# A graph-attention layer and a mixture-of-experts FFN in one kernel: bias and carry matmuls over 128 rows, both square roots behind a relu, two buffers of high halves, two one-hot buffers

## The reference, cut to what matters

```python
x = x + gnn(layernorm(x), edge_attr, W, att_src, att_dst, src, dst)
x = x + ffn(layernorm(x), Wr, br, W1, ..., Wo, bo)

def gnn(feat, dist, ...):                      # 4 heads of 64
    ft = (feat @ W).reshape(n, 4, 64)
    e  = leaky_relu(sum(ft * att_src)[src] + sum(ft * att_dst)[dst], 0.2)
    ex = exp(e - segment_max(e, dst)[dst])
    a  = ex / segment_sum(ex, dst)[dst] * dist
    return segment_sum(ft[src] * a, dst)

def ffn(x, ...):                               # 8 experts, every node goes through all
    w = softmax(x @ Wr + br)
    h = relu(bn(x @ W1[e] + b1[e])); h = relu(bn(h @ W2[e] + b2[e]))
    return sum over e of (h @ Wo[e] + bo[e]) * w[:, e]
```

## Time and profile before

| what | value |
|---|---|
| time, median of 3 runs | 1561.23 us (1560.53 to 1564.69) |
| profiled execution: first to last instruction | 1556.4 us |
| TensorE matmuls busy | 1485.0 us, 95% of the span |
| VectorE busy | 1231.7 us, 79% |
| GpSimd busy | 1063.0 us, 68% |
| ScalarE busy | 742.2 us, 48% |
| mean granted TensorE clock | 0.985 |

### The profile page before, as it was taken

How to read it: one execution, slowest core, us unless ns; L and a number is a source line. 1 busy time by engine, 2 the same in 40 slices (tenths; PEclk the granted TensorE clock), 3 DMA queues, 4 the chain that set the end, 5 groups by cost and what they waited for, 6 DMA issues and landing times.

```text
span 1556.4 us, 24165 instructions
## 1 busy us (share of the span) xinstructions
PE 1485.0 (95%) x8478; PEld 1298.3 (83%) x8478; DVE 1231.7 (79%) x2302; ACT 742.2 (48%) x1293; POOL 1063.0 (68%) x951
## 2 busy tenths in 40 slices
PE   6928999999999999999999999999999999999998
PEld 4727888878888888888888888888888888888887
DVE  7746787887788888878888888888888888888751
ACT  3500444444455555545555555554555555555543
POOL 4176767777778777777777877777777787787000
PEclk9959999999999999999999999999999999999999
DMA  8776344353543444353344444434334444443000
GB/s 239 203 233 192 110 137 124 106 141 94 144 121 111 122 126 127 103 142 108 103 135 118 112 119 118 128 106 137 108 107 134 119 111 119 129 111 91 18 7 8
DMA packets 106070, 187.50 MB, mean 120 GB/s; under 512 B 38357, under 2 KB 70490, under 8 KB 105919
## 3 DMA queue, kind: packets, MB, share of 16 engines
q0 software_dynamic: 44688, 123.13, 28.5%
q1 hardware_dynamic: 60701, 62.29, 13.9%
q10 hardware_dynamic: 560, 0.52, 0.1%
HBM read 172.72 MB, written 14.42 MB: 120 GB/s over the span
## 4 chain that ended last, share of the span: by engine, by line
PE 82%; DVE 9%; DMA 3%; issue 2%; ACT 2%; POOL 1%; SPq 0%; DVEq 0%; ACTq 0%
PE bankH L831 39%; PE bankY L860 21%; PE bankE L783 5%; PE bankE L784 5%; PE bankB L761 3%; PE bankE L776 2%; DVE gath L1431 1%; POOL gath L675 1%; DVE msg_lo L1437 1%; ACT h L1030 1%; DMA table<-gath 1%; PE bankA L808 1%; DVE x L1506 1%; DMA gath<-table,src_win 1%; PE bankA L799 1%
## 5 line engine op out<-in xcount | busy, mean ns | idle before, releaser
L675 POOL DMA_INDIRECT gath<-table,src_win x900 | 1042.5, 1158 | 336.0 <-issue 245.2
L1030 ACT ACTIVATE h<-bankH,bn_shift,bn_scale 128x250 f32<-128x250 f32 x800 | 400.9, 552 | 314.9 <-PE bankH L831 314.7
L831 PE MATMUL bankH<-h,w 128*128 128x250 f32 x1600 | 380.5, 380 | 2.8 <-ACT h L1030 2.1
L860 PE MATMUL bankY<-wo,h 128*125 128x256 f32 x1600 | 378.4, 379 | 1.1 <-DVE x L1506 1.1
L831 PE MATMUL bankH<-xT,w 128*128 128x250 f32 x1600 | 370.9, 374 | 0.3 <-ACT h L1030 0.3
L860 PEld LDWEIGHTS bankY<-wo,h 128*125 128x125 f32 x1600 | 296.1, 187 | 43.2 <-issue 1.4
L831 PEld LDWEIGHTS bankH<-h,w 128*128 128x128 f32 x1600 | 295.6, 191 | 43.4 <-issue 9.6
L831 PEld LDWEIGHTS bankH<-xT,w 128*128 128x128 f32 x1600 | 296.7, 190 | 32.2 <-ACT h L1030 0.4
L1437 DVE TENSOR_TENSOR msg_lo<-gath,msg_hi 128x2340 fp32r<-128x2340 f32 x90 | 234.3, 2603 | 88.0 <-ACT msg_hi L1002 88.0
L1002 ACT ACTIVATE msg_hi<-gath 128x2340 fp32r<-128x2340 f32 x90 | 193.8, 2154 | 217.0 <-PE bankE L784 192.0
L1506 DVE SCALAR_TENSOR_TENSOR x<-bankY,gate,x 125x256 f32<-125x256 f32 x400 | 173.9, 476 | 116.7 <-PE bankY L860 116.1
(11 more groups left out here) (190 smaller groups left out, 1027.6 us busy)
## 6 DMA issues: line engine op xcount, KB each, us to landing
onehot_t<-dst_low SPq DMA_DIRECT2D x48, 576.0 KB, 5.9
gath<-table,src_win POOLq DMA_INDIRECT x900, 2.9
x_res<-in_x SPq DMA_DIRECT2D x25, 250.0 KB
out<-x SPq DMA_DIRECT2D x25, 250.0 KB
table<-gath SPq DMA_DIRECT2D x25, 227.5 KB
w<-in_L_ffn_W SPq DMA_DIRECT2D x8, 512.0 KB
gath<-in_x SPq DMA_DIRECT2D x5, 672.0 KB
wo<-in_L_ffn_Wo SPq DMA_DIRECT2D x4, 512.0 KB
```

The costliest lines, as they stand in the source:

```text
L675: pool.indirect_dma_start(gath[:, g.slot(u), t, :], None, table, bass.IndirectOffsetOnAxis(src_win[:, g.win, u, t:t + 1], 0)).then_inc(row ...
L831: mm = pe.matmul(target[:, hc * 2 * NT:(hc + 1) * 2 * NT], weights[:, e * KC + c, hc * P:(hc + 1) * P], operand(c), start=(c == 0), stop=( ...
L860: mm = pe.matmul(bankY[0:NT, u * D:(u + 1) * D], h2[:, e % 2, c, u, :], wo[:, e * KC + c, :], start=(c == 0), stop=(c == KC - 1))
L1030: ins = act.activation(target[:, e % 2, hc, :, :].rearrange("p u n -> p (u n)"), source[:, hc * 2 * NT:(hc + 1) * 2 * NT], ACT.Relu, bias= ...
```

## The change

- `out_bias` and `turn_carry` work over 128 partitions. `gate_t`, `bo_rows` and `row_max` get 128 rows; the rows that hold nothing are filled once at the start. The carry's transposes now have 128 moving columns instead of 8.
- In the last residual's stage, ScalarE runs relu of layer 2 first and then both `root1`.
- `msg_hi` has two buffers. `keep_high` waits for the chunk before the last one that was split, and `low_part`, whose `msg_lo` still has one buffer, waits for the last one.
- The one-hots have two buffers. Chunks 0 and 1 of pair a are built in stage 7, chunks 2 and 3 of pair g itself in the stages 4 and 5 (3 and 4 in pair 0), each when the chunk two before it has been summed. The code calls these `late`.

```diff
+HOTS = 2
+HIGHS = 2
-NEXT = {4: (0,), 5: (1,), 6: (2,), 7: (3,)}
+NEXT = {7: (0, 1)}
+LATE = {4: (2,), 5: (3,)}
-STEADY = Plan(FOUR, new=2, onehots={4: (0,), 5: (1,), 7: (2, 3)}, residuals={6: (0, 1)}, passes=((0, (0, 1)),), low=ALL)
-PLANS = {0: Plan({2: (0,), 3: (1,), 5: (2,), 6: (3,)}, place=2, new=5, rows=5, onehots={3: (0, 1), 7: (2, 3)},
+STEADY = Plan(FOUR, new=2, onehots=NEXT, late=LATE, residuals={6: (0, 1)}, passes=((0, (0, 1)),), low=ALL)
+PLANS = {0: Plan({2: (0,), 3: (1,), 5: (2,), 6: (3,)}, place=2, new=5, rows=5, onehots={7: (0, 1)}, late={3: (2,), 4: (3,)},
...
-         1: Plan({3: (0,), 4: (1,), 6: (2, 3)}, new=6, rows=6, onehots={4: (0,), 6: (1,), 7: (2, 3)},
+         1: Plan({3: (0,), 4: (1,), 6: (2, 3)}, new=6, rows=6, onehots={7: (0, 1)}, late={4: (2,), 5: (3,)},
...
-def last_low(g, c):
+def low_before(g, c, back):
     for order in reversed(range(g.n * CHUNKS + c)):
         if order % CHUNKS in plan_of(Pair(order // CHUNKS)).low:
-            return order + 1
+            back -= 1
+            if back == 0:
+                return order + 1
     return None
...
-        bo_rows = sb("bo_rows", [4 * EX, D], F32R)
+        bo_rows = sb("bo_rows", [P, D], F32R)
-        onehot = sb("onehot", [P, CHUNKS, TC, NT], F32R)
-        msg_hi = sb("msg_hi", [P, TC, ROW], F32R)
+        onehot = sb("onehot", [P, HOTS, TC, NT], F32R)
+        msg_hi = sb("msg_hi", [P, HIGHS, TC, ROW], F32R)
-        row_max = sb("row_max", [SEG, 2 * P])
+        row_max = sb("row_max", [P, 2 * P])
-        gate_t = sb("gate_t", [4 * EX, 2, NT], F32R)
+        gate_t = sb("gate_t", [P, 2, NT], F32R)
...
-                    mm = pe.transpose(bankC[:, way * SEG:(way + 1) * SEG], row_max[:, way * P:(way + 1) * P], ident[0:SEG, 0:SEG])
+                    mm = pe.transpose(bankC[:, way * P:(way + 1) * P], row_max[:, way * P:(way + 1) * P], ident[:, :])
...
-                if last_low(g, c) is not None:
-                    act.wait_ge(agg_done, last_low(g, c))
+                if low_before(g, c, HIGHS) is not None:
+                    act.wait_ge(agg_done, low_before(g, c, HIGHS))
...
-                    if g is not None and s == max(plan.residuals):
-                        root1(g, 0)
-                        if f is None:
-                            root1(g, 1)
                     if g is not None and s == plan.turn:
                         keep_x1T(g)
                     if run and (s >= 1 or not f.begins(1)):
                         relu2(*before(f, s, 1))
-                    if f is not None and g is not None and s == max(plan.residuals):
+                    if g is not None and s == max(plan.residuals):
+                        root1(g, 0)
                         root1(g, 1)
...
+            own.did(dve.memset(gate_t[:].bitcast(F32), 0.0))
+            own.did(dve.memset(bo_rows[:].bitcast(F32), 0.0))
...
-                if order >= CHUNKS:
-                    dve.wait_ge(agg_done, order + 1 - CHUNKS)
+                if order >= HOTS:
+                    dve.wait_ge(agg_done, order + 1 - HOTS)
...
                 dve.wait_ge(hi_ready, lows(g, c) + 1)
+                if low_before(g, c, 1) is not None:
+                    dve.wait_ge(agg_done, low_before(g, c, 1))
...
-                for c in range(CHUNKS):
+                for c in range(HOTS):
                     make_onehot(a, c)
...
+                    if g is not None:
+                        for c in plan.late.get(s, ()):
+                            make_onehot(g, c)
```

More of the change, by code:

```diff
@@ L87, with __init__ @@
 class Plan:
-    def __init__(self, sums, place=1, bounds=3, new=1, rows=3, onehots=None, residuals=None, products=None, passes=(), low=()):
+    def __init__(self, sums, place=1, bounds=3, new=1, rows=3, onehots=None, late=None, residuals=None, products=None, passes=(), low=()):
         self.sums, self.place, self.bounds, self.new, self.rows, self.onehots = sums, place, bounds, new, rows, onehots
         self.residuals, self.passes, self.low, self.turn = residuals, passes, low, 7
+        self.late = late
         self.products = products or {s - 1: chunks for s, chunks in sums.items()}
@@ L775, in aggregate @@
                     for t in range(TC):
-                        mm = pe.matmul(bankE[u][0:NT, 0:ROW], onehot[:, c, t, :].bitcast(F32), gath[:, g.slot(u), cols + t, :],
+                        mm = pe.matmul(bankE[u][0:NT, 0:ROW], onehot[:, c % HOTS, t, :].bitcast(F32), gath[:, g.slot(u), cols + t, :],
                                        start=(cols + t == 0), stop=(cols + t == TE - 1))
@@ L781, in aggregate @@
                 u, cols = c // 2, (c % 2) * TC
+                high = msg_hi[:, lows(g, c) % HIGHS, :, :]
                 for t in range(TC):
-                    pe.matmul(bankE[u][0:NT, 0:ROW], onehot[:, c, t, :], msg_hi[:, t, :], start=(cols + t == 0), stop=False)
-                    mm = pe.matmul(bankE[u][0:NT, 0:ROW], onehot[:, c, t, :], msg_lo[:, t, :], start=False, stop=(cols + t == TE - 1))
+                    pe.matmul(bankE[u][0:NT, 0:ROW], onehot[:, c % HOTS, t, :], high[:, t, :], start=(cols + t == 0), stop=False)
+                    mm = pe.matmul(bankE[u][0:NT, 0:ROW], onehot[:, c % HOTS, t, :], msg_lo[:, t, :], start=False, stop=(cols + t == TE - 1))
                 mm.then_inc(agg_done, 1)
@@ L998, in keep_high @@
                 act.wait_ge(msg_ready, g.n * CHUNKS + c + 1)
-                if last_low(g, c) is not None:
-                    act.wait_ge(agg_done, last_low(g, c))
+                if low_before(g, c, HIGHS) is not None:
+                    act.wait_ge(agg_done, low_before(g, c, HIGHS))
                 cols = (c % 2) * TC
-                act.activation(msg_hi[:], gath[:, g.slot(c // 2), cols:cols + TC, :], ACT.Copy).then_inc(hi_ready, 1)
+                act.activation(msg_hi[:, lows(g, c) % HIGHS, :, :], gath[:, g.slot(c // 2), cols:cols + TC, :], ACT.Copy).then_inc(hi_ready, 1)
             def exp_logits(g, k, tiles):
@@ L1023, in keep_gate @@
                 act.wait_ge(gateT_done, f.n + 1)
[L1024 removed]
+                act.activation(gate_t[0:4 * EX].rearrange("e u n -> e (u n)"), bankA[0:4 * EX, 256:256 + 2 * NT], ACT.Copy).then_inc(gateT_kept, 1)
             def relu(f, e, l, done, target, source):
@@ L1213, in aside @@
                     own.settle()
-                    dve.scalar_tensor_tensor(bo_rows[:], bo_high.bitcast(F32), bo_pick[:, 1:2], bo_low, ALU.mult, ALU.add).then_inc(bo_ready, 1)
+                    dve.scalar_tensor_tensor(bo_rows[0:4 * EX], bo_high.bitcast(F32), bo_pick[:, 1:2], bo_low, ALU.mult, ALU.add).then_inc(bo_ready, 1)
                 if n == 19:
@@ L1406, in logits @@
                 ends = prefix[:, :, 0:TE:TE - 1]
-                own.did(dve.tensor_tensor(ends, ends, bankC[:, 0:2 * SEG].rearrange("p (k s) -> p s k", k=2), ALU.max))
+                own.did(dve.tensor_tensor(ends, ends, bankC[:, 0:2 * P].rearrange("p (k s) -> p s k", k=2)[:, 0:SEG, :], ALU.max))
                 own.settle()
@@ L1435, in low_part @@
                 dve.wait_ge(hi_ready, lows(g, c) + 1)
+                if low_before(g, c, 1) is not None:
+                    dve.wait_ge(agg_done, low_before(g, c, 1))
                 whole = gath[:, g.slot(c // 2), (c % 2) * TC:(c % 2 + 1) * TC, :]
-                dve.tensor_tensor(msg_lo[:], whole, msg_hi[:].bitcast(F32), ALU.subtract).then_inc(lo_ready, 1)
+                dve.tensor_tensor(msg_lo[:], whole, msg_hi[:, lows(g, c) % HIGHS, :, :].bitcast(F32), ALU.subtract).then_inc(lo_ready, 1)
             def residual(g, u):
```

17 lines of the change are left out of this document (8 added, 9 removed).

## The result

The changed kernel takes 1538.6 us (median of 4 runs, 1534.2 to 1541.0) against 1560.9 us of the kernel before (4 runs, 1557.7 to 1564.7): ratio 0.9856, 95% interval 0.9833 to 0.9879. It is faster by 22.3 us. The forecast was 1544.2 us, 17.0 faster, in a range of 1538 to 1555. The profiled span fell from 1556.4 to 1536.8 us, by 19.6 against a forecast of 17.0.

What follows compares the result with a forecast made beforehand. TensorE was taken as the bound (matmuls 1047.24 of 1050 us). 19 pairs x 0.80 = 15.2 us, last body 0.37 and pairs 0 to 5 1.4 make 17.0: 1561.2 - 17.0 = 1544.2 us, range 1538 to 1555.

Steps and rivals of the forecast that it cites:

- Bias: Bias between two layer blocks, over 128 rows instead of 32: costs 0.24 instead of 0.61 us, gain 0.37 a pair.
- The sign named for it: At the bias: 793.22 to 797.22 becomes 3.63 us long, and L825's weight loads lose their idle.
- padding does nothing: Rival, chance 0.12: the gaps at bias and carry come from something else; 9.6 us fall away, 1553.8 us.
- Carry: Carry ahead of the gate, as two full-row transposes: 0.23 instead of 0.30 us, gain 0.07 a pair.
- Chunks 1 and 2: Layer 3 and sum of these chunks: two buffers make `msg_lo` end 1.9 us earlier, gaining 0.16 and about 0.20 us.
- Roots and chunk 3: Stages 6 and 7, both roots behind the relu: costed at 0, bounds 0 and 0.54 us; stall moves to `turn_x1`.
- The forecast wait: Before `turn_x1` in stage 7: a new wait of line 799 for `xn`, about 0.5 us in 19 pairs.
- the rival that has it go altogether: Rival, chance 0.08: the stall in stage 7 goes altogether, 19 x 0.54 = 10 us more, 1534 us.
- Pairs 0 to 5: Early pairs and the start: one-hots and fills cost +1.2 + 1.5 + 0.3, buffer and rows gain 3.2 and 1.2: -1.4 us.
- The second buffer: Pairs 2 to 5, earlier `msg_lo`: gains 0.6 in pairs 2 and 3, 0.8 in 4, 1.2 in 5: 3.2 us.
- One-hots of stage 7 in pairs 3 and 4: Two built instead of one: idle before `turn_runs` 1.26 instead of 0.53 us, costing 0.73 in each body, 1.5 us.
- The gathers: Rival, chance 0.06: GpSimd's gathers become the bound; at 55.2 us a pair 1552 us, at mean 1.27 nothing gained.

Runs made afterwards that it cites:

- the earlier residual: The changed kernel with VectorE's first residual ahead of the expert sum in stage 6 of the shared plan: 1534.2 us, ratio 0.9835 against the kernel before.

## Why the prediction was right, and where it was off

**Bias: right.** Forecast 0.37 us, measured 0.38, alone and together. The reasoning by distances between starts held: two full-row matmuls cost 0.24 and the rest was the gap. The sign named for it came too: the loads lost their idle time. The rival "padding does nothing" fell with the bias alone, and a gap that goes by the number of rows fell with the 64 rows. What the Trainium skill says in TensorE: Matmul & The Clock Gate (LDWEIGHTS), that a weight load takes as long with 32 rows as with 128, the trace bears out: 0.180 and 0.185 us. That the padding is worth 0 doesn't follow from it, because the price is the idle time ahead of the loads and not their length.

**Carry: right, slightly under.** Forecast 0.07, measured 0.10 in carry and gate, and 0.16 between the pairs of the kernels with and without it. I took two full-row transposes at the price of the gate's two (0.23); they take 0.22 (784.64 - 784.42), and the block ahead of them no longer stands 0.10 longer. That VectorE's answer moves 128 columns instead of 8 cost nothing to be seen.

**Chunks 1 and 2: right.** Forecast 0.16 and 0.20, measured 0.17 and 0.19. `msg_hi` (807.58) starts under the sum that began with the layer 3 of 805.07, and `msg_lo` ends at 812.37, 0.04 after the start of the layer 3 block that precedes its sum, where it had ended 1.66 after it. That is 1.6 us earlier, where 1.9 was forecast; 0.2 would have been enough.

**Roots and chunk 3: the term that was mis-sized.** Forecast 0, measured 0.13 net. The step that failed is "`turn_x1` would stand at 834.32 by TensorE's list and stays at about 834.85 by VectorE's". The last `xn` ended at 834.66, and I took the 0.20 us from there to 834.86 for the cost of handing over. It was not: layer 2 of stage 7 had started late at 833.09, and with 1.77 us, its distance from the transposes in all 17 pairs, TensorE's own list came to 834.86. VectorE's list would have let go earlier. With the roots behind the relu TensorE stands ready and starts 0.05 to 0.06 us after `xn` (827.17 to 827.23). The chain of `xn` itself, which I held to be fixed, was rightly read: it is 7.57 us from layer 3 instead of 7.62. The forecast wait did appear, 19 times, 0.59 us of the weight load each, and the earlier residual shows that it is this chain: with the chain moved up, the stretch is 7.28 us in the middle pair. The stall of 0.54 us was thus worth 0.19 ahead of the transposes and not 0, nor the 0.54 of the rival that has it go altogether.

**The shared pairs' sum.** 19 x 0.80 = 15.2 us were forecast; the 18 bodies of 17.4 us and the sixth body's 1.0 are 18.4. The difference of 3.2 is stage 7 (19 x 0.13 = 2.5) and the rest the carry. The last body's 0.37 came as 0.38 from its layer 1 to layer 3 (1497.56 - 1493.94 = 3.62 us, before 4.00); the 0.3 of the last piece isn't this number, since that piece begins at the bias, behind most of the gap.

**Pairs 0 to 5: right in each mechanism, off in size.** The first five bodies gained 5.1 us and the start lost 4.2, net 0.9 against 1.4. The terms were further off than their sum:

- The second buffer: I took 3.2 us; with one buffer against two the bodies show 5.2. The idle times ahead of `msg_lo` in the kernel before sum to 5.8 there (0.85, 0.85, 0.79, 0.95 and the 2.31 of the earlier trace rows), and nearly all of it was gained.
- One-hots of stage 7 in pairs 3 and 4: I took 0.73 each; alone, the two bodies were 0.76 and 0.77 longer, with the idle of 1.26 that I named. Beside the other parts it is 1.14.
- Bias and carry: I took 1.2; alone, the bias gives 1.1 in these bodies and the carry 1.4.

The parts are not additive here. Each single effect was measured either alone on the kernel before (bias, roots, one-hots) or as the loss without it in the changed kernel (buffer, carry): alone, the roots shorten the fourth body by 1.7 us, and the sum of the single effects (+1.4 - 5.2 - 1.1 - 1.4 - 1.7) is -8.0 us where -5.1 was measured in the same five bodies. Several parts remove the same waiting.

These are the changed kernel's rows beside the earlier trace rows, of TensorE and of VectorE:

```profile
278.97 0.28 PE L749 MATMUL bankC<-ident,prefix 128*8 128x128 f32 x1 [1.14 <-DVE suffix L1375]
...
427.34 2.60 DVE L1445 TENSOR_TENSOR msg_lo<-gath,msg_hi 128x2340 fp32r<-128x2340 f32 x1
```

**The start: open in part.** The first bias came 4.2 us later. VectorE's first moments start at 5.06 instead of 4.62 us. The two fills take 0.54, but three other kernels without them start at 4.79 to 4.93, so by those it is worth 0.1 to 0.3 us. The first gather came 3.25 us later, but it varies: over the profiled executions of all kernels here it starts at 80.2 to 83.5 us, and the first bias at 162.4 to 166.8, 164.1 with the roots alone, which touch nothing at the start. 162.4, the kernel before, is the earliest of them. So some of the 4.2 is chance of the one profile. TensorE's clock differs too. From 80 to 100 us TensorE is busy for 2.4 of the 20 us (1.0 before) and the mean granted clock is 0.55 (0.52 before); from 100 to 120 us it is 0.51, almost all of it at the lower level of 1.2 GHz, where the kernel before had 0.63, and from 80 to 165 us 0.72 against 0.76. Whether the clock makes the start longer or a later start lowers the clock no run here separates. How much the one-hots of pairs 0 and 1 add (I took 1.2) isn't told apart by single profiles; that the one-hots alone cost 5 us in median and only 1.4 in the bodies speaks for more than I took.

**The offset.** I added 4.8 us to the span for the median; the changed kernel's median lies 1.8 above its span. The forecast missed by 5.6 us: 2.6 of them are the span's (19.6 against 17.0) and 3.0 this offset. It compared two different executions: every execution on record takes 1.6 to 2.3 us more than its own span, so the profiled one of the kernel before took some 1558.3 us, 3 less than the median of the first three. With 1.9 for the offset the same sum gives 1541.3.

**The gathers: the rival did not decide, but it was nearer than I held.** I wrote that a pair's gathers take 53 us and fit. The 0.28 us of issue in it spread 178.6 us over all 645 gathers; by the waits of the kernel before it is 0.30 where nothing else is waited for (586 times), and 36 x (1.195 + 0.30) is 54, already near the 54.8 forecast for a pair. In the changed kernel they take 43.6 us and 36 issues of 0.30 us, together 54.5 of a pair of 54.61, and the lead fell from 12.4 to 6.1 us, where it stood still. One gather fewer changed nothing, so the pair is TensorE's and VectorE's; with the pair 0.3 to 0.4 us shorter, the gathers took over once the lead was used up.

## What to carry to other kernels

Take the price of a short matmul amid large ones from the distances between the starts of its neighbours, not from its own length; where a pair of 32-row matmuls costs 0.38 us more than two of 128 rows, rows of zeros are cheaper than few rows. A single buffer between two engines costs where the consumer's last read is the producer's start: look for an idle consumer behind a waiting producer, and count it in the irregular stages as well, where it cost more for each chunk than in the regular ones. When one engine's wait is gone, see which engine has no wait left: here the norms' chain held another 0.3 us a pair (54.61 against 54.3), and right behind it stood the gathers, which had waited 45 us for others before the change.

## What the runs showed of the hardware

**64 rows cost the same gap as 32.** The stretch is 4.01 us against 4.00, and 3.62 with 128.

**A gather is held up by `msg_lo` and hardly by other instructions of VectorE.** Timelines of the changed kernel, GpSimd and VectorE:

```profile
809.99 3.20 POOL L681 DMA_INDIRECT gath<-table,src_win  x1 [0.30 <-issue]
813.49 0.95 POOL L681 DMA_INDIRECT gath<-table,src_win  x1 [0.31 <-issue]
```

```profile
809.77 2.60 DVE L1445 TENSOR_TENSOR msg_lo<-gath,msg_hi 128x2340 fp32r<-128x2340 f32 x1 [0.20 <-ACT msg_hi L1009]
812.28 2.55 DVE L1437 TENSOR_TENSOR gath<-gath,bankC 128x2304 f32<-128x2304 f32 x1
```

The gather that starts under `msg_lo` takes 3.20 us and ends 0.82 after it; the next ones, under the equally long `messages`, take 0.95. In each pair four gathers last over 2 us, as many as there are `msg_lo`; their mean is 3.07 us in the changed kernel and 2.96 before. From 450 us on all 72 of them end 0.82 to 0.83 us behind the end of a `msg_lo`, in both kernels, and no gather that meets no `msg_lo` takes more than 1.35 us. `msg_lo` has two inputs in SBUF, `messages` one in SBUF and one in PSUM. The Trainium skill, SBUF — State Buffer (SBUF: two separate sides), says that a VectorE instruction with two SBUF inputs takes, against a GpSimd instruction that reads SBUF, a port pair which both share, for its whole length. The rows agree with that if a gather counts as such an instruction (its indices `src_win` lie in SBUF); none here varies the inputs alone.

**GpSimd's pace locks to VectorE's.** In the changed kernel the lead of the gathers stayed at 6.1 us over most of the shared pairs, though GpSimd had no wait at all. Each `msg_lo` that catches a gather lets it go 0.82 us behind its own end, and so sets GpSimd's list by VectorE's. The gathers' sum depends on where they are caught, and with few waits it follows the pair: 43.6 us in pairs of 54.61, 43.8 in pairs of 54.77 (narrow carry), 44.0 in pairs of 55.00 (bias over 64 rows). Where GpSimd waits for TensorE it is another one: 42.7 typically in the kernel before, 41.4 in most pairs with one buffer. A sum of issue and mean duration, as I had made it, doesn't hold when the phase changes.
